# Input weights of a state-space scan as products of 16 columns, spread out by VectorE

## The reference, cut to what matters

```
x_ssm = silu(causal_depthwise_conv(split(layernorm(x) @ W_in)[0]))
dt = softplus(x_ssm @ dt_w + dt_b)
Bm = x_ssm @ B_w          # 128 -> 16 states
Cm = x_ssm @ C_w
# scan over the 256 tokens of a sequence, h is 128 channels x 16 states
h = h * exp(dt_t * A)[:, None] + (dt_t * x_t)[:, None] * Bm_t[None, :]
y_t = h @ Cm_t
```

## Time and profile before

| | |
|---|---|
| median of 3 runs | 993.1 us (992.2 to 996.19) |
| profiled execution, its own time | 998.78 us |
| its span, first to last instruction | 997.0 us |
| TensorE busy | 849.1 us, 85% of the span |
| VectorE busy | 677.9 us, 68% |
| ScalarE busy | 565.0 us, 57% |
| GpSimd busy | 446.3 us, 45% |
| granted TensorE clock, mean | 0.866 of full |

### The profile page before, as it was taken

How to read it: one execution, slowest core, us unless ns; L and a number is a source line. 1 busy time by engine, 2 the same in 40 slices (tenths; PEclk the granted TensorE clock), 3 DMA queues, 4 the chain that set the end, 5 groups by cost and what they waited for, 6 DMA issues and landing times.

```text
span 997.0 us, 21501 instructions
## 1 busy us (share of the span) xinstructions
PE 849.1 (85%) x8256; PEld 692.8 (69%) x8256; DVE 677.9 (68%) x1989; ACT 565.0 (57%) x1066; POOL 446.3 (45%) x771
## 2 busy tenths in 40 slices
PE   4887845789999999988766779999999999879995
PEld 4777744668888888867544647877778686767774
DVE  3987863757878788753279957678696868764431
ACT  3553532346667676555566737675867758444541
POOL 1765762323545455345368833435363533340200
PEclk9877875559989898977877769999999999989998
DMA  8300002000000000000000000000000000000000
GB/s 281 99 24 12 24 22 62 26 1 2 2 2 3 1 3 2 2 2 1 0 1 1 1 0 1 1 1 12 1 12 1 12 1 1 11 11 1 12 1 21
DMA packets 22149, 16.76 MB, mean 17 GB/s; under 512 B 2576, under 2 KB 20376, under 8 KB 21792
## 3 DMA queue, kind: packets, MB, share of 16 engines
q1 hardware_dynamic: 21040, 14.77, 4.8%
q10 hardware_dynamic: 1008, 0.63, 0.2%
HBM read 11.20 MB, written 4.19 MB: 15 GB/s over the span
## 4 chain that ended last, share of the span: by engine, by line
PE 60%; DVE 19%; ACT 10%; issue 7%; POOL 3%; DMA 1%; ACTq 0%; POOLq 0%; SPq 0%; DVEq 0%
PE ps L1637 12%; PE ps L1639 8%; PE ps L1638 8%; PE ps L1716 7%; PE ps L1650 6%; PE ps L2063 3%; PE ps L1709 2%; DVE wall L1313 2%; PE ps L1632 2%; DVE vbd L1069 2%; PE ps L1656 2%; PE ps L1938 1%; PE ps L1992 1%; PE ps L1740 1%; DVE a_ln_st L108 1%
## 5 line engine op out<-in xcount | busy, mean ns | idle before, releaser
L1637 PE MATMUL ps<-h_h,wh_h 128*128 128x512 f32 x256 | 109.3, 427 | 16.8 <-ACT h_h L927 8.9
L1638 PE MATMUL ps<-h_h,wh_l 128*128 128x512 f32 x256 | 103.2, 403 | 0.0
L1639 PE MATMUL ps<-h_l,wh_h 128*128 128x512 f32 x256 | 102.9, 402 | 0.0
L1716 PE MATMUL ps<-w_e,he 128*128 128x128 f32 x512 | 88.0, 312 | 3.2 <-ACT he L723 2.9
L723 ACT ACTIVATE he<-ps,pp 128x256 f32<-128x256 f32 x128 | 59.7, 471 | 44.7 <-PE ps L1639 40.4
L1716 PEld LDWEIGHTS ps<-w_e,he 128*128 128x128 f32 x512 | 78.1, 224 | 5.4 <-ACT he L723 4.7
L582 POOL TENSOR_TENSOR term<-term 128x224 f32<-128x224 f32 (+2 forms) x48 | 36.8, 768 | 89.9 <-DVE term L1344 87.4
L1650 PEld LDWEIGHTS ps<-mov,hbd 32*128 32x128 f32 x2048 | 76.2, 227 | 0.0
L1650 PE MATMUL ps<-mov,hbd 32*128 32x32 f32 (+1 forms) x2048 | 75.2, 303 | 0.0
L1637 PEld LDWEIGHTS ps<-h_h,wh_h 128*128 128x128 f32 x256 | 49.9, 195 | 31.0 <-ACT h_h L927 9.9
L117 POOL TENSOR_TENSOR b_ln_ve<-b_ln_mv,eps 128x2 f32<-128x2 f32 x64 | 13.1, 204 | 112.2 <-DVE b_ln_mv L111 112.2
(11 more groups left out here) (292 smaller groups left out, 2527.0 us busy)
## 6 DMA issues: line engine op xcount, KB each, us to landing
x<-in_x SPq DMA_DIRECT2D x16, 128.0 KB
w_h<-in_w_h SPq DMA_DIRECT2D x2, 1024.0 KB, 7.8
x<-x SPq DMA_DIRECT2D x16, 128.0 KB, 1.8
xB<-x SPq DMA_DIRECT2D x32, 64.0 KB
out_x<-xB SPq DMA_DIRECT2D x32, 64.0 KB
w_m<-in_w_m SPq DMA_DIRECT2D x3, 256.0 KB, 5.3
xB<-in_w_e SPq DMA_DIRECT2D x1, 512.0 KB
w_e<-in_w_e SPq DMA_DIRECT2D x1, 512.0 KB
```

Source lines behind the costliest of these rows:

```text
L1637: pe.matmul(dst, a_h, b_h, start=start, stop=True, skip_group_check=True)
L1638: pe.matmul(dst, a_l, b_h, start=False, stop=True, skip_group_check=True)
L1639: return pe.matmul(dst, a_h, b_l, start=False, stop=True, skip_group_check=True)
L1716: last = pe.matmul(ps[:, ACC, P * c:P * c + P], he[e % 2][:, P * c:P * c + P], w_e2[:, e, :], start=False, stop=True, skip_group_check=True)
```

## The change

The moving operand of the products becomes `B_w` itself, 128 x 16: each product gives 16 columns, and the two halves lie next to each other in bank BR, 32 columns in all. VectorE's instruction still writes 512 columns of bbd, but reads each of the 32 PSUM values 16 times in a row (a step of zero) and the 16 values of the mask 32 times over. `w_bR` shrinks from 256 columns to 16, `bmask` from 512 to 16, in SBUF and in what is loaded. No instruction is added, taken away or moved, and all waits stay as they are.

```diff
--- before.py
+++ after.py
@@ -163,11 +163,11 @@
         w_dt = sb("w_dt", [P, D])
         w_b = sb("w_b", [P, BLK])
         w_c = sb("w_c", [P, BLK])
-        w_bR = sb("w_bR", [P, DS, 16])
+        w_bR = sb("w_bR", [P, DS])
         w_cR = sb("w_cR", [P, DS, 8])
         w_conv = sb("w_conv", [P, 4, D])
         w_out = sb("w_out", [P, D])
-        bmask = sb("bmask", [P, 2, DS, 16])
+        bmask = sb("bmask", [P, 16])
         cmask = sb("cmask", [P, NT])
         first = sb("first", [P, NT])
         ones = sb("ones", [P, P])
@@ -326,8 +326,8 @@
             "b": [(rows[:, :, :], "rows"), (stage_f[2][:, :], "c_same"), (stage_f[3][:, :, :], "c_negsel"), (wf[:, :, :], "wf"), (w_router[:, :], "w_router"), (w_e1[:, :, :], "w_e1"), (w_e2[:, :, :], "w_e2"),
                   (b_e2[:, :], "b_e2"), (router_b[:, :, :], "router_b"), (iota[:, :], "c_iota")],
             "c": [(w_in[:, :], "w_in"), (w_dt[:, :], "w_dt"), (w_b[:, :], "w_b"), (w_c[:, :], "w_c"),
-                  (w_conv[:, :, :], "conv_r"), (w_bR[:, :, :], "w_bR"), (w_cR[:, :, :], "w_cR"), (w_out[:, :], "w_out"),
-                  (bmask[:, :, :, :], "c_bmask"), (cmask[:, :], "c_cmask"), (first[:, :], "c_first")],
+                  (w_conv[:, :, :], "conv_r"), (w_bR[:, :], "w_bR"), (w_cR[:, :, :], "w_cR"), (w_out[:, :], "w_out"),
+                  (bmask[:, :], "c_bmask"), (cmask[:, :], "c_cmask"), (first[:, :], "c_first")],
             "d": [(w_m1[:, :], "w_m1"), (w_m2[:, :], "w_m2"), (w_h1[:, :, :], "w_h1"), (w_h2[:, :, :], "w_h2"),
                   (w_m3[:, :, :], "w_m3"), (w3_s[:, :, :], "w3_s")],
         }
@@ -1414,7 +1414,9 @@
 
             def inputs_by_chunk(t):
                 dve.wait_ge(S["c_br_ps"], t + 1)
-                dve.tensor_tensor(flat3(bbd[t % 2][:, :, :]), ps[:, BR, :], bmask[:, :, :, :].rearrange("p k n c -> p (k n c)"),
+                rows_by_state = lambda v: v.to_broadcast([P, 2 * DS, 16])
+                dve.tensor_tensor(flat3(bbd[t % 2][:, :, :]).rearrange("p (n c) -> p n c", c=16),
+                                  rows_by_state(ps[:, BR, 0:2 * DS].unsqueeze(2)), rows_by_state(bmask[:, :].unsqueeze(1)),
                                   ALU.mult).then_inc(S["c_bbd"], 1)
 
             def fill(n):
@@ -1956,7 +1958,7 @@
 
                     pe.wait_ge(S["d_yr"], t // 2 - 3)
                 for c in range(2):
-                    last = pe.matmul(ps[:, BR, NT * c:NT * c + NT], xs[t % 2][:, P * c:P * c + P], flat3(w_bR[:, :, :]),
+                    last = pe.matmul(ps[:, BR, DS * c:DS * c + DS], xs[t % 2][:, P * c:P * c + P], w_bR[:, :],
                                      start=True, stop=True)
                 last.then_inc(S["c_br_ps"], 1)
 
@@ -2219,7 +2221,7 @@
     for m in ("w_b", "w_c"):
         r[m] = np.concatenate([r[m], np.zeros((D, BLK - DS), f)], 1)
     r["conv_r"] = np.broadcast_to(v["L1_attn_conv_w"][:, 0, :].T[None, :, :], (P, 4, D))
-    r["w_bR"] = np.broadcast_to(v["L1_attn_B_w"][:, :, None], (D, DS, 16))
+    r["w_bR"] = v["L1_attn_B_w"]
     r["w_cR"] = np.broadcast_to(v["L1_attn_C_w"][:, :, None], (D, DS, 8))
     r["w_m1"], r["w_m2"] = v["L1_ffn_w1_w"].T, v["L1_ffn_w2_w"].T
     for n, k in (("w_h1", "h1_w"), ("w_h2", "h2_w"), ("w_m3", "w3_w")):
@@ -2238,7 +2240,7 @@
     e = np.arange(NE)
     r["c_negsel"] = np.where(e[:, None, None] == e[None, :, None], 0.0, NEG).astype(f) * np.ones((1, 1, P), f)
     r["c_iota"] = np.broadcast_to(e.astype(f), (P, NE))
-    r["c_bmask"] = np.broadcast_to((p[:, None] // CH == np.arange(16)[None, :]).astype(f)[:, None, None, :], (P, 2, DS, 16))
+    r["c_bmask"] = (p[:, None] // CH == np.arange(16)[None, :]).astype(f)
     t = np.arange(NT)[None, :]
     r["c_cmask"] = (p[:, None] % 8 == t // CH // 4).astype(f)
     r["c_first"] = np.broadcast_to((np.arange(NT) % CH != 0).astype(f), (P, NT))
```

## The result

The changed kernel takes 1002.28 us, the median of 21 runs (997.49 to 1008.64). The kernel before, run beside it 21 times, has a median of 996.89 (989.31 to 1002.02); its first three runs, from which the forecast took 993.1, lay low in that scatter. The ratio is **1.0065 [1.0042, 1.0088]**: slower by 0.65%, where 0.16% faster was forecast, and outside the range. The profiled execution took 1003.2 us with a span of 1001.4.

The account below looks back on a forecast made before the run. TensorE, busy for 85% of the span and 60% of the chain, was taken as the bound. Saving 2.9 us and giving back 1.3 made -1.6 us, so 993.1 became 991.5 us, range 987.5 to 997.5.

Parts of the forecast that it names:

- I count two falls in five where there was one: 1.3 us given back: TensorE's clock halving after the lengthened first-gelu waits, 600 to 818 us: one more fall, costing 1.3 us.
- The bound of 5.2 us: Upper bound of that clock cost: falls in all five periods, 5.2 us lost.
- The clock falls in all five periods: Rival: half clock after the first-gelu wait in every period, four more falls, 5.2 us, giving 995.4 us; 13%.
- a way to lose a fall (15%): Rival: periods shift against whatever sets the clock and the one fall goes, giving 988.9 us; 15%.
- The products' term: Narrower TensorE products save 0.49 us at each of six places on the chain, 2.9 us in all.
- The gain doesn't arrive: Rival: small products cost more, or the 2.9 us become idle time behind the next latest work, giving 994.4 us; 10%.
- VectorE's term: VectorE's bbd product, reading each PSUM value 16 times, stays at 0.69 us: 0 more.
- Loads and placement: Smaller w_bR and bmask loads and SBUF tiles moving down by some 3 KB per partition: nothing gained or lost.
- The base: Time of the kernel before that the forecast started from: 993.1 us, median of the runs.
- the clock's term: TensorE clock falls in the five periods from 600 to 818 us: 1.3 us given back in the sum.

Follow-up runs that it names:

- narrow_ahead: Changed kernel with the old large w_bR and bmask, 16 columns only at t = 6, 8, 10, 12, 14, 256 elsewhere: 1.0062 of the kernel before.
- first_only: Changed kernel with the old large w_bR and bmask, 16 columns only at t = 0 to 5, 256 elsewhere: 1.0025 of the kernel before.
- late_only: Changed kernel with the old large w_bR and bmask, 16 columns only at t = 7, 9, 11, 13, 15: 1.0034 of the kernel before.
- late_and_twice: As late_only, but the 256-column products of t = 6, 8, 10, 12, 14 moved into TensorE's wait for ScalarE and issued twice: 0.9984 of the kernel before.
- narrow_wide_tiles: Changed kernel, 16 columns everywhere, with w_bR and bmask as large in SBUF and loads as before the change: 1.0102 of the kernel before.
- after_again: The changed kernel unaltered, timed and profiled a second time: 1.0088 of the kernel before.
- twice_in_wait: As late_and_twice, but with 16 columns at t = 0 to 5 too: 1.0025 of the kernel before.
- filled: late_and_twice with the products repeated three times more in steps n = 1 to 3, in TensorE's wait for VectorE: 0.9996 of the kernel before.
- all_wide: Changed kernel with the old large w_bR and bmask and 256 columns everywhere, VectorE still reading with a step of zero: 1.0018 of the kernel before.

## Why the prediction was wrong

**What failed is one step**: "I count two falls in five where there was one: 1.3 us given back". There were five of five, two of them twice as long, and one more behind the segment. The term is (23.9 - 3.4) x 0.43 = 8.8 us in the segment and 1.4 behind it, where 1.3 stood in the sum. The same thing happened at the border, where the sum had no term for the clock at all: t = 0's products save their 0.5 us, yet the border is 1.0 longer in the changed kernel's profile. The bound of 5.2 us was too low as well, since it allowed one stretch per wait. That the clock was the danger, and the main place of it, was right: the rival "The clock falls in all five periods" came, with 13%, and with too small a price.

Why I counted low: I interpolated between the lengths of two waits, 1.78 and 2.56 us, as if the length decided. It does not alone. In narrow_ahead a wait of 2.20 us was followed by a fall twice in five, in first_only one of 1.78 never, in late_only one of 1.78 three times. The one fall before was not a chance of one in five that a longer wait raises a little: three kernels with the same waits and columns in the segment had none, one and two, and the shorter period alone went with as many (10.2 us of half time) as the longer wait alone (10.2). The text named the second alone, and gave the shift of the periods only as a way to lose a fall (15%).

**The products' term was right**: -0.49 us a place. The records went from 0.86 to 0.35 (0.51), and the five places of the segment gave 2.2 us once the falls are taken out; first_only and late_and_twice show it as 270.9 against 268.7. The rival "The gain doesn't arrive" is refuted for four of the five, whose periods are 0.5 us shorter in spite of the 0.40 us of the earlier trace rows; in the fifth only 0.15 arrives. At t = 0 the 0.5 us arrives at the next long wait (11.34 us for 11.85) and is then lost to the clock in the border. The Trainium skill, "TensorE: Matmul & The Clock Gate", section on LDWEIGHTS, led to an estimate of 0.43 us for four records; they took 0.35, 88 ns each, so the trace does not follow it at this point.

**VectorE's term was right**: 0 more, 0.689 us. The Trainium skill, "Vector Engine (DVE) Microarchitecture Reference", section 5.2, which measures operands in SBUF, read to the letter, gave an estimate of 0.35 us more for an operand whose neighbours aren't adjacent words. A PSUM word repeated 16 times runs at the full rate here, 0.689 us, so this case gives no sign that a step of zero counts as such a hop.

**Loads and placement: nothing that slows**, as forecast (narrow_wide_tiles). One difference is left open: from `from_states` of t = 0 to that of t = 1 both profiles of the changed kernel take 15.5 us, and every kernel with the large tiles 16.3 to 16.7.

**The base was off too**: 993.1 is the median of three runs, and 21 runs give 996.89. That moves the number by 3.8 us, not the sign. The error in the difference is 7.0 us by the medians (+5.4 against -1.6) and 6.0 by the two profiled executions (+4.4). In the profiles it splits as follows: the clock's term was 8.8 + 1.4 - 1.3 = 8.9 too small, and the border 1.5 (1.0 longer, where 0.5 shorter stood in the sum). Against that stand 2.9 us less from t = 0 to 4 and 2.1 less ahead of t = 0's products, which the change doesn't reach; 0.6 is left over. Of the 2.9, 1.2 is the open difference above, and 1.6 is the step to t = 4, whose clock was higher.

The clock's share holds beyond the profiled executions. In the runs of after_again, on one chip, the mean granted clock is 0.8583, against 0.8717 for the kernel before. That is 2 x 0.0134 x 1000 = 27 us more at half clock, times 0.43 is 11.5, less the 2.9 that the forecast has as saved is 8.6, against 8.8 measured (1.0088). This is a rough estimate, since it prices all half time as if it lay on TensorE's chain.

**What stays open.** What makes the clock fall at a given wait is described here, not explained: that the change's two halves together bring it down is shown, how each works isn't. Nor is it shown how to bank the 2.2 us: the kernels with narrow odd places and no fall in the segment are 1.0025 (twice_in_wait), 0.9984 (late_and_twice) and 0.9996 (filled) of the kernel before. For twice_in_wait the border is a likely reason, 3.4 us longer in its profile; late_and_twice avoids that and is 1.6 us faster than before by its ratio, with an interval of 3.4 us either way. No version beat the kernel before by more than its interval, and none kept t = 0 wide with a single product in the wait.

## What to carry to other kernels

When a kernel holds TensorE's clock just barely, work taken off TensorE has two prices: its own time on the chain, and the clock that it helped to hold; here 2.2 us saved came with 8.8 lost. Where a period shows a fall in one of five repetitions, a forecast should price the fall in every repetition, with double stretches, before it counts the saving, and look at every other long wait behind a shortened product too, as at the border here. If such a product must go, look for harmless work to put into the wait behind it (not ahead of it, where it delays the chain), and expect nothing from a higher clock in stretches where another engine sets the pace. That filler keeps the clock is shown here; that it makes this kernel faster than before is not.

## What the runs showed of the hardware

- The same wait of 1.78 us for ScalarE was followed by half clock in none, one or two of five periods with the same 256 columns in both steps of a period (first_only, before, all_wide), and in three with 16 columns in the other step (late_only).
- A product of 16 moving columns costs 88 ns a record on the chain where one of 256 costs 215 (0.35 and 0.86 us for four).
- Two products of 16 columns in place of 256, some 6 us ahead of a wait of 5.20 us, went with 34.1 us at half clock where wide ones had 17.1, in two kernels of six; in the other four it was 13.7 to 20.5 (first_only, twice_in_wait and the rows there).
- VectorE multiplies a PSUM operand and an SBUF operand, both with repeated or cyclic reads, at 689 ns for 512 columns, no slower than straight ones.
- A TensorE clock of 1.00 instead of 0.75 over 50 us saved 0.1 us where VectorE was busy for 97% of the time (filled, late_and_twice).
